# A wait for the last scatters' landing added on GpSimd, at the end of a GNN and mixture-of-experts kernel

## What is computed

```python
def _L0_ffn_ref(x, rw1, rb1, rw2, rb2, ew1, eb1, ew2, eb2):
    ...
    vals, idx = jax.lax.top_k(logits, K)
    ...
    w = jax.nn.softmax(masked, axis=1)
    eh = jax.nn.silu(jnp.einsum('td,edh->teh', t, ew1) + eb1[None])
    eo = jnp.einsum('teh,ehd->ted', eh, ew2) + eb2[None]
    y = t + jnp.einsum('te,ted->td', w, eo)
    return y.reshape(b, f, d)
x = x + _L0_gnn_ref(_layernorm(x, axis=-1), src, dst, ...)
x = x + _L0_ffn_ref(_layernorm(x, axis=-1)[None], ...)[0]
```

## Time and profile before

| what | us |
|---|---|
| median of 3 runs | 1116.31 |
| the 3 runs | 1115.01, 1116.31, 1117.41 |
| the profiled execution, its own time | 1116.28 |
| span of its trace, first to last instruction | 1114.5 |
| PE busy in it | 1056.4 |
| GpSimd busy in it | 190.7 |

### The profile page before, as it was taken

One profiled execution on the slowest core, in us unless ns is written; L12 is line 12 of the kernel. 1 busy time (PEld: TensorE's weight loads), 2 busy tenths in 40 slices (PEclk: granted clock), 3 DMA queues, 4 the chain that ended last, 5 costly groups with the idle time before them and its releaser, 6 DMA issues.

```text
span 1114.5 us, 17998 instructions
## 1 busy us (share of the span) xinstructions
PE 1056.4 (95%) x6444; PEld 1008.8 (91%) x6444; DVE 621.9 (56%) x1090; ACT 427.9 (38%) x934; POOL 190.7 (17%) x192
## 2 busy tenths in 40 slices
PE   4999999999989999999999999999999579999995
PEld 3999999999989999999999999999999469999994
DVE  6668888888743354324333442274222468878883
ACT  5555444443311222112121112164223257767772
POOL 5500000000000002000200020002443124454432
PEclk9999999999989999999999999999999759999998
DMA  6322133213126651004300430176655087999981
GB/s 192 92 94 72 51 109 107 66 44 107 70 71 187 200 162 40 1 2 134 98 1 15 144 98 1 38 238 185 182 169 207 6 306 244 314 308 288 306 223 29
DMA packets 72793, 144.95 MB, mean 130 GB/s; under 512 B 12822, under 2 KB 51667, under 8 KB 68209
## 3 DMA queue, kind: packets, MB, share of 16 engines
q1 hardware_dynamic: 61041, 112.50, 31.6%
q0 software_dynamic: 10976, 30.74, 10.8%
q10 hardware_dynamic: 672, 0.32, 0.1%
HBM read 108.40 MB, written 42.96 MB: 136 GB/s over the span
## 4 chain that ended last, share of the span: by engine, by line
PE 87%; DVE 4%; issue 3%; PEld 2%; DMA 1%; ACT 1%; DVEq 1%; POOLq 0%; SPq 0%; ACTq 0%; POOL 0%; PEldq 0%
PE ps L1460 20%; PE ps L937 14%; PE ps L1532 10%; PE ps L2098 9%; PE ps L1191 9%; PE ps L1499 8%; PE ps L2119 6%; PE ps L809 4%; PE ps L2084 2%; PEld ps L733 2%; PE ps L905 1%; DVE key_hot L802 1%; DVE adj L816 1%; PE ps L1518 1%; PE ps L911 1%
## 5 line engine op out<-in xcount | busy, mean ns | idle before, releaser
L1422 POOL TENSOR_TENSOR s_rows<-s_rows,b1t 125x1368 f32<-125x1368 f32 (+3 forms) x9 | 23.7, 2652 | 579.5 <-DMA s_rows<-in_x 579.5
L816 DVE TENSOR_TENSOR adj<-ps,adj 125x250 f32 x212 | 88.0, 415 | 41.8 <-PE ps L809 33.6
L937 PE MATMUL ps<-h_lo,w_hi 128*128 128x418 f32 x336 | 108.6, 372 | 0.0
L937 PE MATMUL ps<-h_hi,w_hi 128*128 128x418 f32 x336 | 100.4, 380 | 0.0
L1499 PE MATMUL ps<-z_hi,adj 125*125 125x342 f32 (+1 forms) x300 | 95.0, 322 | 1.2 <-DVE s_rows L1731 1.2
L1499 PE MATMUL ps<-z_lo,adj 125*125 125x342 f32 (+1 forms) x300 | 94.4, 320 | 0.6 <-issue 0.6
L937 PE MATMUL ps<-h_hi,w_lo 128*128 128x418 f32 x336 | 93.5, 360 | 0.0
L2189 DVE TENSOR_TENSOR w_lo<-w_raw,w_hi 128x2048 fp32r<-128x2048 f32 x34 | 77.8, 2289 | 25.5 <-ACT w_hi L2144 22.0
L1191 PE MATMUL ps<-adj,y_hi 125*128 125x416 f32 (+1 forms) x240 | 86.6, 361 | 3.8 <-issue 3.4
L1191 PE MATMUL ps<-adj,y_lo 125*128 125x416 f32 (+1 forms) x240 | 86.2, 359 | 1.4 <-issue 1.4
L809 PE MATMUL ps<-key_hot,src_hot 125*125 125x250 bf16 x424 | 80.9, 272 | 3.3 <-DVE adj L816 3.0
(11 more groups left out here) (299 smaller groups left out, 2664.9 us busy)
## 6 DMA issues: line engine op xcount, KB each, us to landing
w_raw<-in_L_ffn_ew SPq DMA_DIRECT2D x34, 1024.0 KB, 8.0
xin<-in_x SPq DMA_DIRECT2D x10, 448.0 KB
t_d<-xn SPq DMA_DIRECT2D x10, 448.0 KB
base<-x_d POOLq DMA_DIRECT2D x10, 448.0 KB, 4.2
out<-base POOLq DMA_DIRECT2D x10, 448.0 KB, 3.4
y_d<-y_hi SPq DMA_DIRECT2D x7, 625.0 KB
y_d<-y_lo SPq DMA_DIRECT2D x7, 625.0 KB
self_d<-self SPq DMA_DIRECT2D x7, 625.0 KB
```

The lines of the kernel that those rows point to most:

```text
L816: e.tensor_tensor(cols, ps[0:P, 5 + b % 2, 0:KW].rearrange("p (t w) -> p t w", t=NT), cols, ALU.add).then_inc(self.took, 1)
L937: mm = e.matmul(BANK(m, own, c), wt[:, own, k, :], ht[:, k, a:a + w], start=(k == 0 and p == 0), stop=(k == KT - 1 and p == 2))
L1422: e.tensor_tensor(cols, cols, b1t[:, 0:w].rearrange("p (a n) -> p a n", a=1).to_broadcast([P, n, w]), ALU.add).then_inc(s_x, 1)
```

## The change

GpSimd gets the four waits that SP has, behind its last scatter and ahead of the block's end:

```diff
@@ -2233,6 +2233,12 @@
                 for b in range(SUB):
                     e.wait_ge(m_st[u][b], NTH(NS - 1 - (NS - 1 - u) % 2, b))
 
+        @on("gpsimd")
+        def _(e):
+            for u in range(2):
+                for b in range(SUB):
+                    e.wait_ge(m_st[u][b], NTH(NS - 1 - (NS - 1 - u) % 2, b))
+
         with nc.Block() as block:
             for engine, parts in ((block.sync, prog["sync"]), (block.scalar, prog["scalar"]),
                                   (block.vector, prog["vector"]), (block.gpsimd, prog["gpsimd"]),
```

## The result

| | median us | runs | lowest to highest |
|---|---|---|---|
| before | 1119.23 | 20 | 1115.01 to 1130.30 |
| changed | 1123.90 | 20 | 1118.87 to 1130.56 |

The ratio of the changed kernel to the one before is 1.0048, with a 95% interval of 1.0030 to 1.0067. So it is slower, by 5.4 us on 1119 (3.4 to 7.5). A second comparison, with executions of its own, gave 1.0044 (1.0009 to 1.0080). The table's kernel before is also 2.9 us above the 1116.31 of the first three runs: single executions of both kernels spread over 12 to 15 us.

The account below looks back on a forecast made before the run. TensorE sets nearly the whole span, GpSimd's last DRAIN the tail. DRAIN start 1109.8 + 4.7 = 1114.5 against 1114.31, 0.2 us more; 1116.28 + 0.2 = 1116.5 us. Own range 1114.2 to 1117.6, whole range 1111.5 to 1119.9.

Parts of the forecast that it names:

- What bounds the tail: Block's end: GpSimd's DRAIN, 1104.78 to 1114.31 us, ends last; nothing upstream of 1105 changes.
- The added waits themselves: GpSimd's queue: three waits already true, 0.05 us hidden; the fourth starts the DRAIN at about 1109.8, 5.0 us later.
- What I take, X = 4.7 us: Length of GpSimd's last DRAIN once the scatter has landed: 4.7 us, ending at 1114.5, 0.2 us more.
- The argument for it: GpSimd's last DRAIN ends 4.7 us behind the 1109.6 landing, so some work or slow look wasn't spared by the landing.
- the first rival: Block's end: a DRAIN started behind the landing takes 0.2 us, so the tail goes, 4.3 us less, 1112.0; chance 0.30.
- the second rival: Block's end: the DRAIN's own work, hidden by the scatter's flight, gets serialized; 3.3 or 5.0 us more; chance 0.22.
- its nearer case: GpSimd's last DRAIN takes 7.76 us, counted from the last scatter row's end; 3.3 us more, 1119.6; chance 0.16.
- The third rival: Block's end: something independent of the DRAIN, timed from the scatter's issue, ends at 1114.3; no change, 1116.3; chance 0.07.
- the first DRAIN: GpSimd's own first DRAIN, before any DMA was issued on it, took 0.187 us; held against hidden DRAIN work.

Follow-up runs that it names:

- The second DRAIN: Changed kernel with one more GpSimd DRAIN between the added waits and the block's own DRAIN; the two DRAINs took 7.745 and 0.040 us.
- the kernel with 188 since the program's start: Changed kernel with 94 small GpSimd DMAs more, issued in the graph layers, and no DRAIN between; last DRAIN 7.752 us.
- the one of step 8: Kernel before plus DRAINs ahead of the expert stage and behind the landing waits in scatters of steps 8, 13, 14, 15; ratio 1.0020, step 8's DRAIN 9.311 us.
- one early DRAIN: Kernel before, without the added wait, plus one GpSimd DRAIN ahead of the expert stage; ratio 0.9981 (0.9954 to 1.0008).
- three in flight: Kernel before plus DRAINs ahead of the expert stage and ahead of the landing waits in scatters of steps 13, 14, 15; ratio 0.9999 (0.9971 to 1.0027).
- two DRAINs: Kernel before, without the added wait, plus DRAINs ahead of the expert stage and at the start of step 14's scatter; ratio 0.9981 (0.9957 to 1.0005).

## Why the prediction was wrong

The direction was wrong and so was the range: no change was forecast, 1116.5 us, and 1123.9 was measured, above the upper end of 1119.9.

- *What bounds the tail:* right. GpSimd's DRAIN ends last in both kernels, and nothing ahead of the last scatter's row was touched.
- *The added waits themselves:* right. The DRAIN starts 0.1 us behind the landing, where 0.2 was taken from SP's rows.
- *What I take, X = 4.7 us:* this is the step that failed. X is 7.747. I took the 4.7 us behind the landing for work that the landing sets off. The runs show that it was the rest of work of 7.745 us, 0.082 us for each of 94 DMAs issued since the last DRAIN, that had begun at the end of the last scatter's row. The second DRAIN's 0.040 us, the 4.471 us for 54 DMAs and the 10.202 for 124 show it. The added wait puts the part that lay beside the flight, 3.1 to 3.4 us, behind it.
- *The argument for it:* "if the DRAIN only had to learn that the DMA is over, it would now end just behind 1109.6" is true, but it excludes only the first rival. I let it speak for the forecast as well, while it spoke for the second rival as much.
- *The rivals:* the second was right, and its nearer case to 0.02 us (7.76 worked out, 7.747 measured), down to its mechanism of going through what was issued. It had 0.16. What I held against it, that the first DRAIN shows no such work, was no evidence: as I wrote there, nothing had been issued by then. The first rival is out, since a DRAIN is short when there is nothing new (0.040 us) but not when everything has merely landed. The Trainium skill's sentence in "PSUM — Partial Sum Buffer", section "Engine vs sequencer instructions", that a drain waits for its engine to be fully idle, agrees with the 0.040 us and tells nothing of the 7.745.
- *The third rival* is out by the changed profile itself: counted from the end of the last scatter's row, the DRAIN ended 11.3 us later (1118.7 + 7.747 - 1115.16) and not 7.76. Something timed from the scatter's issue would have ended where it did before.
- *The range:* its upper end was the second rival's 1119.6 for an execution like the profiled one. The spread of runs was put at 1 us, from three runs that lay within 2.4. Over 20 runs the same kernel spans 15 us, and its median is 2.9 higher. The tail's 3.5 us on 1119.23 give 1122.7, and that also lies above 1119.9.
- *The size:* the tail explains 0.31% of the measured 0.48, and lies just inside its interval (from 0.30) and well inside that of the second comparison. Whether there is more isn't shown; no profile has it.

## What to carry to other kernels

Don't put a wait for DMAs ahead of an instruction that may have work of its own to do in the meantime: here the wait cost the whole overlap. When a stretch of a DRAIN behind a landing is unexplained, count how much of it may be work by number and not by time, and ask when it began; one more DRAIN right behind it tells a price per DRAIN from a price for what has piled up. A DRAIN in an earlier idle time shortens the last one's tail, but look for who waits behind it and for DMAs still in flight; that any of these kernels is faster isn't shown.

## What the runs showed of the hardware

Where all of GpSimd's DMAs have landed when it starts, a GpSimd DRAIN took 0.082 to 0.083 us for each DMA that GpSimd had issued since its last DRAIN, large or small, direct or indirect, landed 670 us ago or just now: 94 in 7.745, 54 in 4.471, 124 in 10.202 us. The one exception is the kernel with 188 since the program's start, which took 7.752. With a DMA in flight a DRAIN can take longer than that: 15.092 us for 48, 9.311 us for 34.

Half of the price seems to be paid only when the last DMA has landed. If the work is two passes of 0.041 us per DMA, of which the first can't end ahead of the last landing, then the DRAINs would be over at the times of this table (an estimate). It is a fit to rows that were there, made afterwards, and no run was made to test it. It would explain the two DRAINs that ended 2.0 us behind a landing, and the one of step 8 fits roughly: 34 x 0.041 = 1.4 us, and it ended at 1031.4, 1.9 us behind the last packet at 1029.5. Its gather's landing has no time in the trace.

| DRAIN | DMAs | could start | landing | worked out | measured |
|---|---|---|---|---|---|
| kernel before, last | 94 | 1106.55 | 1109.6 | 1106.55 + 3.87 + 3.87 = 1114.29 | 1114.31 |
| one early DRAIN, last | 54 | 1109.11 | 1112.26 | 1112.26 + 2.22 = 1114.48 | 1114.45 |
| three in flight, step 13 | 48 | 1085.56 | 1094.4 | 1094.4 + 1.98 = 1096.4 | 1096.4 |
| two DRAINs, step 14 | 49 | 1090.51 | 1095.25 | 1095.25 + 2.02 = 1097.27 | 1097.25 |
